# A graph network layer stack on one core: three-bank PSUM rings and one TensorE semaphore per step

## The reference

```python
ew = edge_attr @ edge_w + edge_b                        # (100000, 32) @ (32, 256)
rel_masks = [(edge_type == i).astype(x.dtype) for i in range(3)]
inv_cnt = [1.0 / jnp.maximum(segment_sum(m, dst), 1.0) for m in rel_masks]
for l in range(3):
    residual = x
    msg = relu(x[src] * ew)                             # a gather of 100000 rows of 1 KB
    out = 0
    for i in range(3):
        h = segment_sum(msg * rel_masks[i][:, None], dst) * inv_cnt[i][:, None]
        out = out + h @ weights[l, i]
    out = out + x @ roots[l] + biases[l]
    x = residual + relu(out)
return layernorm(x_in + x)
```

## Time and profile before

| | us |
|---|---|
| timed, median of 3 | 2964.37 |
| span of the profiled execution | 3581.6 |
| POOL busy in it | 2224.3 (62%) |
| TensorE busy | 2843.8 (79%) |
| VectorE busy | 2148.4 (60%) |
| ScalarE busy | 1289.4 (36%) |

### The profile page before, as it was taken

One profiled execution on the slowest core, in us unless ns is written; L12 is line 12 of the kernel. 1 busy time (PEld: TensorE's weight loads), 2 busy tenths in 40 slices (PEclk: granted clock), 3 DMA queues, 4 the chain that ended last, 5 costly groups with the idle time before them and its releaser, 6 DMA issues.

```text
span 3581.6 us, 59909 instructions
## 1 busy us (share of the span) xinstructions
PE 2843.8 (79%) x18436; PEld 2613.2 (73%) x18436; DVE 2148.4 (60%) x6028; ACT 1289.4 (36%) x2738; POOL 2224.3 (62%) x2364
## 2 busy tenths in 40 slices
PE   6888888888888877787777877777777777787777
PEld 6777777777777777777777777767777777776776
DVE  5666666666666555555555555555556656665665
ACT  5555555555555322222222222222222222222222
POOL 6666666666666566666666666656666666666664
PEclk9999999999999888888898889988888888899898
DMA  6554555555455444444444444444444444444443
GB/s 148 135 137 132 137 135 138 136 137 137 131 137 145 133 120 127 125 130 127 126 127 127 134 124 127 131 127 132 126 124 128 125 127 131 125 130 124 128 128 99
DMA packets 334989, 465.42 MB, mean 130 GB/s; under 512 B 158995, under 2 KB 221646, under 8 KB 334670
## 3 DMA queue, kind: packets, MB, share of 16 engines
q0 software_dynamic: 112608, 307.65, 30.1%
q1 hardware_dynamic: 221244, 153.70, 15.6%
q10 hardware_dynamic: 818, 0.18, 0.0%
HBM read 403.94 MB, written 57.36 MB: 129 GB/s over the span
## 4 chain that ended last, share of the span: by engine, by line
PE 59%; issue 17%; DVE 9%; another core or an unknown queue 8%; ACT 4%; DVEq 2%; DMA 0%; ACTq 0%
PE bank L911 29%; PE bank L867 14%; PE bank L961 12%; DVE acc L1138 4%; PE bank L846 2%; DVE xg L1300 1%; ACT oh_a L812 1%; DVE t L1155 1%; ACT at L753 1%; DVEq L1274 1%; PE bank L936 1%; DVEq L1138 1%; ACT xg L791 1%; DVE S L1097 1%
## 5 line engine op out<-in xcount | busy, mean ns | idle before, releaser
L700 POOL DMA_INDIRECT xg<-x,idx x1540 | 1457.0, 946 | 870.6 <-issue 351.7
L911 PE MATMUL bank<-S,xg 128*128 128x96 f32 x9384 | 1450.5, 304 | 360.3 <-issue 176.3
L911 PEld LDWEIGHTS bank<-S,xg 128*128 128x128 f32 x9384 | 1313.6, 216 | 429.2 <-issue 385.4
L791 ACT ACTIVATE xg<-xg 128x512 f32<-128x512 f32 x1170 | 736.7, 630 | 2102.3 <-DVE xg L1300 1193.8
L1300 DVE TENSOR_TENSOR xg<-xg,bank 128x512 f32<-128x512 f32 x1170 | 800.8, 684 | 691.0 <-remote 329.4
L1138 DVE TENSOR_TENSOR acc<-acc,bank 128x192 f32 x2346 | 816.7, 348 | 570.0 <-PE bank L911 343.0
L867 PE MATMUL bank<-wsb,at 128*128 128x256 f32 x4692 | 985.7, 337 | 213.6 <-issue 123.3
L700 POOL DMA_INDIRECT xg<-in_x_dram,idx x782 | 742.2, 949 | 454.2 <-PE bank L911 211.2
L867 PEld LDWEIGHTS bank<-wsb,at 128*128 128x128 f32 x4692 | 749.3, 214 | 297.6 <-issue 195.9
L961 PE MATMUL bank<-W,acc 128*128 128x256 f32 (+1 forms) x1764 | 515.9, 415 | 7.2 <-issue 6.4
L961 PEld LDWEIGHTS bank<-W,acc 128*128 128x128 f32 (+1 forms) x1764 | 386.9, 258 | 17.3 <-issue 12.1
(11 more groups left out here) (75 smaller groups left out, 789.7 us busy)
## 6 DMA issues: line engine op xcount, KB each, us to landing
at<-attr_t SPq DMA_DIRECT2D x390, 128.0 KB
attr_t<-at SPq DMA_DIRECT2D x195, 128.0 KB
xg<-x,idx POOLq DMA_INDIRECT x1540
xg<-in_x_dram,idx POOLq DMA_INDIRECT x782
hs<-in_edge_attr_dram SPq DMA_DIRECT2D x194, 64.0 KB
x<-t SPq DMA_DIRECT2D x96, 128.0 KB
xblk<-x SPq DMA_DIRECT2D x96, 128.0 KB
y<-t SPq DMA_DIRECT2D x94, 128.0 KB
```

Source lines behind the costliest of these rows:

```text
L700: eng.indirect_dma_start(out=xg[:, n % XR, :], out_offset=None, in_=rows_in, in_offset=bass.IndirectOffsetOnAxis(ap=rows_at, axis=0)).then ...
L791: eng.activation(v, v, ACT.Relu).then_inc(s_r, 1)
L911: last = eng.matmul(sums_bank(l, q, i)[:, 192 * i + 96 * h:192 * i + 96 * h + 96], xg[:, n % XR, 128 * h:128 * h + 128], S[:, slot(l, 2 * ...
```

## The change

Both shared PSUM rings become three banks deep, and TensorE's signals are merged.

- `pA` is now banks 2, 3 and 5, `pE` banks 0, 1 and 4. The third banks were `pT` (turned attributes and turned `x`) and the bank that held the numbers 0 to 147 for the comparisons; these numbers now stand in the free columns of the three `pA` banks.
- `add_sums` runs three steps after the multiply instead of two; `edge_weights` is emitted two steps ahead instead of one. Turned `x` and the last block's products take turns in the `pE` ring (`users`, `free_shared_bank`).
- `s_sc` is raised once per step, at the second tile (at a layer's last step once per tile), and `s_e` only in steps 0 to 2 of a layer. From step 3 on, whoever needs the edge weights of step `q` waits for the sums of step `q - 3` (`wait_edges`).
- The attributes arrive already turned, as a new input `attr_2` (twice the 32 rows), so `attr_turn` and `attr_copy` go: one load of 128 KB a group, one ScalarE copy straight into `at`, one VectorE subtraction over 32 partitions x 512 instead of 128 x 128.
- VectorE copies the counts of a block to `kept` (49 copies of three columns), and TensorE's `count` reads them there; its waits for `s_inv` and VectorE's for `s_cm` go.

The core of the diff:

```diff
-        pE = bank[0:2]
-        pA = bank[2:4]
+        pE = [bank[0], bank[1], bank[4]]
+        pA = [bank[2], bank[3], bank[5]]
...
+        def collected(l, q):
+
+            return l * (NP + 1) + q + 1 + (q == NP - 1)
+
+        def wait_edges(eng, l, q):
+
+            if q < 3:
+                eng.wait_ge(s_e, 3 * l + q + 1)
+            else:
+                eng.wait_ge(s_sc, collected(l, q - 3))
...
+        def free_shared_bank(eng, what, l, i):
+
+            before = turn_of[what, l, i] - 3
+            if before < 0:
+                return
+            what, l, i = users[before]
+            if what == "edges":
+                eng.wait_ge(s_m, l * NP + i + 1)
+            elif what == "turned":
+                eng.wait_ge(s_xc, NB * l + i + 1)
+            else:
+                eng.wait_ge(s_f0, NB * l + i + 1)
...
             def load_attr(g):
-                if g >= 3:
-                    eng.wait_ge(s_tr, g - 2)
...
+                if g >= HR2:
+                    eng.wait_ge(s_lo, g - HR2 + 1)
+                a, w = 128 * head_tile(order[g]), 128 * tiles_of(g)
+                eng.dma_start(hs[0:64, g % HR2, 0:w], attr_2[:, a:a + w]).then_inc(s_an[g % HR2], 16)
...
                 if n >= XR:
-                    eng.wait_ge(s_sc, 2 * ((n - XR) // 2 + 1))
+                    eng.wait_ge(s_sc, collected(*divmod((n - XR) // 2, NP)))
...
-                eng.activation(hs[:, g % 3, :, 0:32].bitcast(F32R), hs[:, g % 3, :, 32:64], ACT.Copy).then_inc(s_hi, 1)
-
-            def attr_copy(g):
...
-                eng.activation(at[0:64, g % TR, 0:w], pT[0:64, 0:w], ACT.Copy).then_inc(s_atc, 1)
+                eng.activation(at[0:64, g % TR, 0:w], hs[0:64, g % HR2, 0:w], ACT.Copy).then_inc(s_hi, 1)
...
-            def attr_turn(g):
...
-                for i in range(tiles_of(g)):
-                    last = eng.transpose(pT[0:64, 128 * i:128 * i + 128], hs[:, g % 3, i, :], ident[:, :])
-                last.then_inc(s_tr, 1)
...
-                last.then_inc(s_e, 1)
+                if q < 3:
+                    last.then_inc(s_e, 1)
...
-                    last.then_inc(s_sc, 1)
+                    if i or q == NP - 1:
+                        last.then_inc(s_sc, 1)
...
-                        if (1 if l else 0) <= q < NP - 1:
-                            edge_weights(l, q + 1)
+                        if (0 if l else -1) <= q < NP - 2:
+                            edge_weights(l, q + 2)
...
-                raw, high = hs[:, g % 3, :, 32:64], hs[:, g % 3, :, 0:32]
+                w = 128 * tiles_of(g)
                 eng.wait_ge(s_hi, g + 1)
-                eng.tensor_tensor(raw, raw, high, ALU.subtract).then_inc(s_lo, 1)
+                eng.tensor_tensor(at[32:64, g % TR, 0:w], hs[32:64, g % HR2, 0:w],
+                                  at[32:64, g % TR, 0:w].bitcast(F32), ALU.subtract).then_inc(s_lo, 1)
...
-                            eng.wait_ge(s_e, Q + 1)
+                            wait_edges(eng, l, q)
...
-                        if 0 <= q - 2 < NP:
-                            add_sums(l, q - 2, 1)
+                        if 0 <= q - 3 < NP:
+                            add_sums(l, q - 3, 1)
```

More of the change, by code:

```diff
@@ L264, in turn_step @@
         def turn_step(k):
[L266 removed]
+            return starts[k] - (3 if k < NB - 1 else 7)
         def mix_step(l, k, m):
@@ L309, in slot @@
             return 4 * ((l * NQ + j // 4) % (SR // 4)) + j % 4
-        end = starts[-1] + 16
         heads = 12
```

241 lines of the change are left out of this document (128 added, 113 removed).

## The result

The changed kernel takes 2997.59 us (median of 4 runs, 2997.25 to 2999.86), the kernel before 2964.33 us (4 runs beside them). The ratio is 1.0111, 95% interval 1.0097 to 1.0125: 33 us slower, outside the range forecast. In a second series it was 1.0086 (1.0073 to 1.0100), 26 us.

The account below looks back on a forecast made before the run. POOL's issue of gathers was taken as the bound before and after. Its part and both ends gave 2963.6 us, the change -1 for the attributes and 0 for the rest: 2963 us from the timed median, range 2946 to 2978.

Parts of the forecast that it names:

- What bounds the kernel: POOL issues gathers almost without a pause, 1.252 us each; with both ends 2963.6 us against 2964.37 timed.
- the 617 us: Profiled span over timed median, laid to TensorE's signals arriving 2 to 3.5 us late, of which timed runs have little.
- The sign that I had set for it: A profiled span that shortens with no gain in the timed run would settle that the 618 us were the profiler's.
- Fewer signals: On TensorE, some 2300 signal increments fewer; value 0, since TensorE's savings are not on POOL's path.
- The estimate of 61 us: 2300 increments at 26 ns each, less on TensorE; time would fall by that only if TensorE set the pace.
- Three banks and lags: PSUM rings let TensorE and VectorE be a step later; POOL's waits stay the same: cost and gain 0.
- The attributes: Layer 0: TensorE loses 131.3 us of turning, VectorE's wider subtraction adds 0.15 us per step, both hidden; taken as 1 us.
- rule on the held start: VectorE's subtraction on partitions 32 to 63 and its follower would lose overlap: 2.18 us per step, without it 2.10.
- Borders and start: At the start and the two layer borders, where POOL waits: between 3 us less and 3 us more, taken as 0.
- B: Rival: TensorE's late signals hold the timed run too, so 2840 us or below; chance 0.13.
- C: Rival: TensorE paces stretches of layer 0 and a ring of three hides it, 2957 us; chance 0.12.
- D: Rival: VectorE becomes the bound of layer 0 when its added work passes 2.50 us per step, 2983 us; chance 0.14.

Follow-up runs that it names:

- 8 columns: Changed kernel with the subtraction over 8 columns in place of 512, all else kept: ratio 1.0043, 12.8 us over the kernel before.
- the kernel before with one signal: Kernel before with TensorE's signal for the sums raised once per step and not twice, waits counted accordingly: ratio 1.0003.
- the halves: Changed kernel with the same subtraction as two of 256 columns: ratio 1.0073, 21.7 us over the kernel before.
- the quarters: Changed kernel with the same subtraction as four of 128 columns: ratio 1.0061, 18.1 us over the kernel before.
- the one operand: Changed kernel with the subtraction right behind the comparison: second input from PSUM 2977.03 us, both inputs from SBUF 2997.78 us.
- the changed kernel with remedies: Changed kernel with subtraction in four parts, two attribute loads asked for earlier, layer 0's first edge-weight multiplication doubled: 1.0044 on the chip with late signals.

## Why the prediction was wrong

*What bounds the kernel.* Right: POOL's issue, 2346 gathers at a pitch of 1.250 us, with both ends, holds before and after. But the reason given for the 617 us was wrong. I took the late signals for the profiler's; one chip here has them in timed runs as well (3539.39 us timed, profiles of 3534.6 us and up). So the trace of before, 3581.6 us long, was most likely taken on such a chip and the times on another; which chip it was isn't known. The sign that I had set for it, a profiled span that shortens with no gain in the timed run, did come (2995.6 us) and would have misled: the profile was simply of a chip with prompt signals. All four times of the series forecast were on such a chip, so the sum came out for a wrong reason, which is luck.

*Fewer signals.* Right in size: 1.0003 for half of the increments of `s_sc`. The estimate of 61 us from the Trainium skill's figure (TensorE: Matmul & The Clock Gate, "The cost: per-tile semaphore tail") was for all 2300 increments. Half of them are gone in this run, and of the 30 us that are its share of the estimate nothing is seen in the time. It would be seen only if TensorE set the pace, as said in the prediction. What the merged `s_e` does by itself wasn't tried.

*Three banks and lags.* Valued at nothing. With the clash taken away (8 columns) 12.8 us stay over the kernel before, of which the profile shows 2.1 at the start, 3.3 at the first border and 2.9 at the second; the rest is open, and its profiled execution was 5 us shorter than the median of its times. The steady part costs nothing: the pitches up to 1.3 us are 1.250 us in the mean, 1.253 and 1.2505 in the two traces of the kernel before with one signal.

*The attributes.* This is the step that failed. "VectorE gets a subtraction of 512 columns", +0.15 us per step, hidden below POOL's 2.50, with all gathers left at 0.946 us; those of layer 0 took 0.972. The duration of the subtraction was off by 0.085 us only (0.685 against 0.60), and VectorE stays below POOL at 2.25 us per step (2.10 to 2.18 forecast; of the 0.30 more, 0.20 are the longer subtraction, about 0.08 the overlaps lost below, 0.02 the copies). But I had asked only whether VectorE had room, not what the instruction does to the engine that is the bound while it runs. It was there to be seen: 53 gathers of the trace before are some 40 ns longer under the old subtraction, both of whose inputs lie in SBUF too. With 0.285 us the gathers over 0.96 us were 2.7 us too long there; the cost grows about with the square of what exceeds 0.13 us, as a longer instruction catches more gathers and holds each for longer (an estimate that gave 24, 12 and 6 us for the whole, the halves and the quarters, against 20.5, 12.7 and 7.2). This alone is 17 to 18 us more than in the kernel before in the profiles, and about 20 of the 33 in the timed runs (20.8 for the one operand, 3.6 of them at the first border).

By the Trainium skill's rule on the held start (VectorE: DVE Perf Modes, "Two Vector instructions with no wait between them") the new subtraction loses the overlap. The trace agrees: from its start at 47.47 to the next at 48.18 are 0.71 us, its whole length and 0.03, and it starts 0.23 us behind one of 0.19. Back to back, others start 0.08 us before the last one has ended; the second half of the subtraction, on the same partitions as the first, does so by 0.07.

*Borders and start.* "Between 3 us less and 3 us more; I take 0." Mis-sized: 2.8 us more at the start than in the kernel before with one signal (4.71 against 1.92), 3.6 at the first border, 2.6 at the second. I had looked for instructions added on the chain, and not at what a ring of two slots does to a load in SP's queue, nor at TensorE's clock. Of the three, the start and the second border are tied to a cause by an edit that moved them in the changed kernel; the first isn't.

*The rivals.* B is refuted where the times were taken, and on the chip where its premise holds there was no gain either for the changed kernel with remedies (1.0044). C is refuted: what waits were left (11.9 us in pitches over 1.3 us) didn't go but grew. D forecast the right side by the wrong way: splitting the subtraction gave VectorE more work and the kernel less time. The rival that was missing: a slower POOL, by what VectorE reads.

Adding up: clash 17.4 us more than in the kernel before with one signal, start 2.8, borders 3.6 and 2.6, together 26.4 of the 30.7 us by which all pitches over 1.3 us grew, where 33.3 us were measured in one series and 25.6 in another. The 8 us between the two series are more than any single term but the clash, so the small terms rest on the profiles, not on the timed ratios.

## What to carry to other kernels

When one engine is the bound, ask of each instruction that is added elsewhere not only whether its own engine has room, but what it shares with the bound: on VectorE, whether both inputs lie in SBUF while GpSimd starts a gather. One input in PSUM, or several short instructions for a long one, cost VectorE about the same or more here and the kernel less. A group whose mean moves by 2% while the instruction is untouched is worth a look at its longest members.

And hold a profile whose span is far from the median against a second profile before a reason is given for the difference.

## What the runs showed of the hardware

- A gather of 128 rows that starts 0.045 us or more into the subtraction with two SBUF inputs is longer by what is left of it less 0.13 us (0.39 for 0.52; 69 gathers, to within 0.01). With one input in PSUM it isn't (layer 0 at 949 ns in the mean with a subtraction of 679 ns; 0.946 us under the multiply).
- A gather that starts earlier isn't lengthened; within 0.045 us of the subtraction's start it is the subtraction that grows, from 0.681 to as much as 0.76 us.
- The same program takes 2965 to 2972 us in the median on four chips and 3539 on another, where TensorE's sums reach the engines that wait for them 1.3 to 1.5 us after their end in the place shown. There POOL waits for the sums, and 17.6 us of longer gathers don't show in the time (0.9995).
- In the changed kernel, which took 131 us of work from TensorE in layer 0, TensorE is at half clock for 126 us there in place of 38 (kernel before with one signal), and over all three layers for 441 in place of 236. With one multiplication per step put back it was 76 us in layer 0.
